# Four of sixteen feed-forward weight products as seven products of 2x2 blocks in a fused transformer layer

## The reference

```
y   = layernorm(x)
sa  = selfattention(y);          a = ln1(y + sa)
ca  = crossattention(a, ctx);    b = ln2(a + ca)
ff  = relu(b @ w1.T + b1) @ w2.T + b2            # 512 -> 2048 -> 512
x   = x + ln3(b + ff)
z   = layernorm(x)
out = x + gate(z) * (relu(z @ W1) @ W2)          # 512 -> 2048 -> 512
```

## Time and profile before

| | |
|---|---|
| median of 3 runs | 531.16 us (529.92 to 531.4) |
| the profiled execution | 530.6 us, span 528.8 us |
| TensorE matmul busy | 518.0 us, 98% of the span |
| VectorE busy | 325.5 us, 62% |
| ScalarE busy | 222.3 us, 42% |
| GpSimd busy | 103.4 us, 20% |

### The profile page before, as it was taken

One profiled execution on the slowest core, in us unless ns is written; L12 is line 12 of the kernel. 1 busy time (PEld: TensorE's weight loads), 2 busy tenths in 40 slices (PEclk: granted clock), 3 DMA queues, 4 the chain that ended last, 5 costly groups with the idle time before them and its releaser, 6 DMA issues.

```text
span 528.8 us, 7550 instructions
## 1 busy us (share of the span) xinstructions
PE 518.0 (98%) x3018; PEld 495.4 (94%) x3018; DVE 325.5 (62%) x558; ACT 222.3 (42%) x388; POOL 103.4 (20%) x92
## 2 busy tenths in 40 slices
PE   7999999999999999999999999999999999999997
PEld 6899999789988878999999999999999899999996
DVE  3743788895698986877365544277684364442225
ACT  3853542383688866264535163206413331320200
POOL 1430430122032135054006300005530000000000
PEclk9999999999999999999999999999999999999999
DMA  8951212031599971229022222002220033100004
GB/s 228 334 187 57 74 64 79 1 113 56 193 292 321 309 219 38 79 96 228 1 77 83 81 81 79 1 0 81 81 79 1 0 126 115 53 28 0 1 1 124
DMA packets 18443, 53.75 MB, mean 102 GB/s; under 512 B 1640, under 2 KB 2440, under 8 KB 15848
## 3 DMA queue, kind: packets, MB, share of 16 engines
q1 hardware_dynamic: 18348, 53.20, 31.2%
q10 hardware_dynamic: 60, 0.07, 0.1%
HBM read 51.63 MB, written 1.64 MB: 101 GB/s over the span
## 4 chain that ended last, share of the span: by engine, by line
PE 81%; DVE 9%; DMA 4%; ACT 3%; issue 1%; SPq 1%; DVEq 0%; ACTq 0%
PE ps L572 21%; PE ps L574 21%; PE ps L573 21%; PE ps L626 3%; DMA OR<-wvo_in 2%; PE ps L602 2%; PE ps L765 1%; DMA cnR<-ctxn_in 1%; PE ps L767 1%; PE ps L766 1%; DMA ctR<-ctxt_in 1%; DVE cnL L1194 1%; PE ps L637 1%; PE ps L739 1%; PE ps L741 1%
## 5 line engine op out<-in xcount | busy, mean ns | idle before, releaser
L572 PE MATMUL ps<-XH,WH 128*128 128x400 f32 x352 | 122.5, 348 | 0.8 <-DVE AL L1206 0.4
L574 PE MATMUL ps<-XH,WL 128*128 128x400 f32 x352 | 121.5, 345 | 0.0
L573 PE MATMUL ps<-XL,WH 128*128 128x400 f32 x352 | 121.4, 345 | 0.0
L572 PE MATMUL ps<-AH,WH 128*128 128x400 f32 x284 | 98.7, 348 | 0.6 <-DVE AL L1210 0.2
L574 PE MATMUL ps<-AH,WL 128*128 128x400 f32 x284 | 98.0, 345 | 0.0
L573 PE MATMUL ps<-AL,WH 128*128 128x400 f32 x284 | 97.9, 345 | 0.0
L572 PEld LDWEIGHTS ps<-XH,WH 128*128 128x128 f32 x352 | 66.1, 188 | 2.7 <-DVE AL L1206 0.8
L573 PEld LDWEIGHTS ps<-XL,WH 128*128 128x128 f32 x352 | 66.2, 188 | 0.0
L574 PEld LDWEIGHTS ps<-XH,WL 128*128 128x128 f32 x352 | 66.2, 188 | 0.0
L484 POOL TENSOR_TENSOR WL<-WR,WH 128x512 fp32r<-128x512 f32 x38 | 52.4, 1410 | 66.6 <-ACT WH L919 66.6
L572 PEld LDWEIGHTS ps<-AH,WH 128*128 128x128 f32 x284 | 53.3, 188 | 2.1 <-DVE AL L1210 1.9
(11 more groups left out here) (188 smaller groups left out, 826.6 us busy)
## 6 DMA issues: line engine op xcount, KB each, us to landing
...
cnR<-ctxn_in SPq DMA_DIRECT2D x8, 256.0 KB
...
VR<-wvo_in SPq DMA_DIRECT2D x4, 256.0 KB, 6.4
```

Of the source, the lines that this page charges most:

```text
L572: pe.matmul(dst, wh, half(mh, h, k), start=(k == 0), stop=False)
L573: pe.matmul(dst, wh, half(ml, h, k), start=False, stop=False)
L574: mm = pe.matmul(dst, wl, half(mh, h, k), start=False, stop=(k == KC - 1))
```

## The change

Four up units (9, 11, 19, 21) are each computed by seven block products instead of eight (the Winograd form of Strassen's scheme). The weights are a 2x2 grid of 256 x 256 blocks, and the tokens' two halves times two feature halves are the other 2x2 grid. POOL makes four sums of weight blocks (`sum_blocks`) for each such unit and, once for each feed forward, four sums of feature blocks (`sum_features`). ACT and DVE split them in high and low parts, at the places that `BLOCKS_AT` and `SUMS_AT` name. One of PE's `strassen(n)` runs 7 products x 2 groups x 6 matmuls; ACT copies the first product out of PSUM, DVE makes the sums of the products in AT and `mid`, ACT writes AH with relu, DVE AL, in the order `HANDED`.

With it go:
- In the first feed forward ORDER becomes 7,0 8,0 7,1 8,1 9 10,0 10,1; before it was 7,0 8,0 9,0 7,1 8,1 9,1 10,0 10,1. The transposes to features of the second half move from after group 0 of 9,0 to after group 1 of 8,0.
- The full-precision normed features are kept in XF, so unit 8's residual is one DVE operation. For the second feed forward eight ACT copies out of PSUM write XF (`copy_features`), and the next transposes or gating rows wait for them.
- The weights of 10, 12, 20 and 22 are split at other places (`MOVED`). POOL's eight additions to the input tokens wait for the end of unit 11 rather than of unit 9. SP's loads of input tokens, g3 and be3 wait for the first four block sums. The load after a block unit waits for its four sums and three low halves.

```diff
-        ORDER += [(_up[0], 0), (_down[0], 0), (_up[1], 0), (_up[0], 1), (_down[0], 1), (_up[1], 1),
+        ORDER += [(_up[0], 0), (_down[0], 0), (_up[0], 1), (_down[0], 1), (_up[1], 0), (_up[1], 1),
...
+STRASSEN = (U_F + 2, U_F + 4, U_M + 4, U_M + 6)
+PRODUCTS = 14
+MOVED = {U_F + 3: POS[U_F + 2, 0], U_F + 5: POS[U_F + 3, 1], U_M + 5: POS[U_M + 3, 1], U_M + 7: POS[U_M + 5, 1]}
...
+BLOCKS_AT = {(U_F, 1): (U_F + 2, [[], [], [0, 1, 2], [3, 4]]), (U_F + 1, 1): (U_F + 2, [[5, 6], [], [], []]),
+             (U_F + 3, 0): (U_F + 4, [[0, 1], [2, 3], [4], [5]]), (U_F + 3, 1): (U_F + 4, [[6], [], [], []]),
+             (U_M + 2, 1): (U_M + 4, [[0, 1], [2], [3], [4]]), (U_M + 3, 0): (U_M + 4, [[5], [6], [], []]),
+             (U_M + 5, 0): (U_M + 6, [[0, 1], [2, 3], [4, 5], [6]])}
+SUMS_AT = {(U_F + 1, 1): (0, [[], [0], [1], [2, 3]]),
+           (U_M + 1, 1): (1, [[0], [1], [2], []]), (U_M + 3, 0): (1, [[], [], [3], []])}
+HANDED = [(0, 0), (0, 1), (0, 2), (0, 3), (1, 2), (1, 3), (1, 0), (1, 1)]
+WHOLE = [n for n in LOADED if n not in STRASSEN]
...
+        def blocks(n, i):
+            if i >= 4:
+                x = n == U_M + 6
+                return [w[x][:, i - 4, :, :] for w in (WXH, WXL, WXS)]
+            ks, es = [(0, 0), (2, 0), (2, D // 2), (0, D // 2)][i]
+            return [w[SLOT[n]][:, ks:ks + 2, es:es + D // 2] for w in (WH, WL, WS)]
+        def raw_block(ks, es):
+            return WR[:, 2 * ks:2 * ks + 2, es * D // 2:(es + 1) * D // 2]
+        def sums(t):
+            lo, whole = [w[0][:, 2 * t:2 * t + 2, :] if t < 3 else w[1][:, :, :] for w in (TL, TS)]
+            return TH[:, 2 * t:2 * t + 2, :], lo, whole
+        def product(n, i, e):
+            return gemm_count(n, 0, 2 * i + e)
...
+            sp.wait_ge(block_sum, 4)
...
+            def sum_blocks(n):
+                pool.wait_ge(weights_loaded, 16 * LOADED.index(n))
+                if BEFORE[n] is None:
+                    pool.wait_ge(c_attT, B)
+                    pool.wait_ge(ct_low, 2 * B)
+                else:
+                    pool.wait_ge(gemm_done, gemm_through(BEFORE[n]))
+                if n == U_F + 4:
+                    pool.wait_ge(gemm_done, gemm_through(U_F + 2))
+                done = 4 * STRASSEN.index(n)
+                a11, a12, a21, a22 = raw_block(0, 0), raw_block(1, 0), raw_block(0, 1), raw_block(1, 1)
+                s2, s3, s1, s4 = [blocks(n, i)[2] for i in range(3, 7)]
+                pool.tensor_tensor(s1, a21, a22, ALU.add).then_inc(block_sum, 1)
+                pool.wait_ge(block_sum, done + 1)
+                pool.tensor_tensor(s2, s1, a11, ALU.subtract).then_inc(block_sum, 1)
+                pool.wait_ge(block_sum, done + 2)
+                pool.tensor_tensor(s4, a12, s2, ALU.subtract).then_inc(block_sum, 1)
+                pool.tensor_tensor(s3, a11, a21, ALU.subtract).then_inc(block_sum, 1)
+            def sum_features(f):
+                if f == 0:
+                    pool.wait_ge(x_ready, 24)
+                else:
+                    pool.wait_ge(x_copied, 2 * KC)
+                b11, b21 = XF[0][:, 0:2, :], XF[0][:, 2:4, :]
+                b12, b22 = XF[1][:, 0:2, :], XF[1][:, 2:4, :]
+                t2, t3, t4, t1 = [sums(t)[2] for t in range(4)]
+                pool.tensor_tensor(t1, b12, b11, ALU.subtract).then_inc(feature_sum, 1)
+                pool.wait_ge(feature_sum, 4 * f + 1)
+                pool.tensor_tensor(t2, b22, t1, ALU.subtract).then_inc(feature_sum, 1)
+                pool.wait_ge(feature_sum, 4 * f + 2)
+                pool.tensor_tensor(t4, t2, b21, ALU.subtract).then_inc(feature_sum, 1)
+                pool.tensor_tensor(t3, b22, b12, ALU.subtract).then_inc(feature_sum, 1)
...
-            split_weights(U_F + 2)
+            sum_blocks(U_F + 2)
+            sum_features(0)
+            sum_blocks(U_F + 4)
             pool.wait_ge(xres_loaded, 32)
             pool.wait_ge(gb_loaded, 32)
-            pool.wait_ge(gemm_done, gemm_count(U_F + 2, 1, KC - 1))
+            pool.wait_ge(gemm_done, gemm_through(U_F + 4))
...
+            sum_features(1)
+            sum_blocks(U_M + 4)
+            sum_blocks(U_M + 6)
...
+                    elif pn in STRASSEN:
+                        if e < 2:
+                            pe.wait_ge(before_relu, 8 * STRASSEN.index(pn) + e + 3)
+                        else:
+                            pe.wait_ge(two_summed, 2 * STRASSEN.index(pn) + e - 1)
...
+            def strassen(n):
+                at = STRASSEN.index(n)
+                pn, ph = ORDER[POS[n, 0] - 1]
+                f = int(n >= U_M)
+                def b(h, k):
+                    return XH[h][:, k:k + 2, :], XL[h][:, k:k + 2, :]
+                moving = [b(0, 0), b(0, 2), sums(0), sums(1), sums(2), sums(3), b(1, 2)]
+                for i in range(7):
+                    ah, al = blocks(n, [0, 1, 3, 4, 2, 5, 6][i])[:2]
+                    bh, bl = moving[i][:2]
+                    for e in range(2):
+                        dst = ps[:, [4, 0, 2, 6, 0, 4, 6][i] + e, 0:HALF]
+                        if e == 0:
+                            pe.wait_ge(block_low, 7 * at + [1, 2, 4, 5, 5, 6, 7][i])
+                            if 2 <= i < 6:
+                                pe.wait_ge(feature_low, 4 * f + i - 1)
+                            else:
+                                pe.wait_ge(x_ready, 24 + 8 * f)
+                        if i in (0, 3) and f == 1:
+                            pe.wait_ge(g_shift, 2)
+                            pe.wait_ge(g_rows_sb, 2)
+                        if i in (0, 3) and at >= 1:
+                            pe.wait_ge(before_relu, 8 * at)
+                        elif i == 1:
+                            pe.wait_ge(dve_evac, dve_count(pn, ph, e))
+                        elif i == 2:
+                            pe.wait_ge(dve_evac, dve_count(pn, ph, 2 + e))
+                        elif i == 4:
+                            pe.wait_ge(before_relu, 8 * at + e + 1)
+                        elif i == 5:
+                            pe.wait_ge(first_copied, 2 * at + e + 1)
+                        elif i == 6:
+                            pe.wait_ge(three_summed, 2 * at + e + 1)
+                        cols = slice(e * P, (e + 1) * P)
+                        for k in range(2):
+                            pe.matmul(dst, ah[:, k, cols], bh[:, k, :], start=(k == 0), stop=False)
+                            pe.matmul(dst, ah[:, k, cols], bl[:, k, :], start=False, stop=False)
+                            mm = pe.matmul(dst, al[:, k, cols], bh[:, k, :], start=False, stop=(k == 1))
+                        mm.then_inc(gemm_done, 1)
...
-            unit(U_F + 1, 0)
-            unit(U_F + 2, 0, [0])
+            unit(U_F + 1, 0, [0, 1])
             to_features(2, 1, xn[1])
-            unit(U_F + 2, 0, [1, 2, 3])
-            for n, h in ORDER[POS[U_F, 1]:POS[U_M - 3, 1]]:
-                unit(n, h)
+            unit(U_F + 1, 0, [2, 3])
+            units(ORDER[POS[U_F, 1]:POS[U_M - 3, 1]])
...
+                    if (n, h) in SUMS_AT:
+                        f, here = SUMS_AT[n, h]
+                        for t in here[e]:
+                            act.wait_ge(feature_sum, 4 * f + (3 if t == 0 else 4))
+                            hi, _, whole = sums(t)
+                            act.activation(hi, whole, ACT.Copy).then_inc(feature_high, 1)
+                    if (n, h) in BLOCKS_AT:
+                        m, here = BLOCKS_AT[n, h]
+                        for i in here[e]:
+                            split_block(m, i)
+            def split_block(n, i):
+                at = STRASSEN.index(n)
+                hi, _, src = blocks(n, i)
+                if i < 3:
+                    act.wait_ge(weights_loaded, 16 * LOADED.index(n))
+                    if BEFORE[n] is None:
+                        act.wait_ge(c_attT, B)
+                        act.wait_ge(ct_low, 2 * B)
+                    else:
+                        act.wait_ge(gemm_done, gemm_through(BEFORE[n]))
+                    src = raw_block([0, 1, 1][i], [0, 0, 1][i])
+                else:
+                    act.wait_ge(block_sum, 4 * at + (3 if i == 3 else 4))
+                act.activation(hi, src, ACT.Copy).then_inc(block_high, 1)
+            def strassen(n):
+                at = STRASSEN.index(n)
+                for e in range(2):
+                    act.wait_ge(gemm_done, product(n, 0, e))
+                    act.activation(mid[:, e, :], ps[:, 4 + e, 0:HALF], ACT.Copy).then_inc(first_copied, 1)
+                for p in range(2):
+                    if POS[n, p] in SPLIT_AT:
+                        for k in range(KC):
+                            split_weights(SPLIT_AT[POS[n, p]], k)
+                for i, (h, e) in enumerate(HANDED):
+                    act.wait_ge(before_relu, 8 * at + i + 1)
+                    act.activation(half(AH, h, e), half(AT, h, e), ACT.Relu).then_inc(act_evac, 1)
...
```

(90 more changed lines are left out.)

89 lines of the change are left out of this document (66 added, 23 removed).

## The result

The changed kernel takes 522.83 us (median of 4, 522.34 to 523.88) against 530.65 us (4 runs, 529.92 to 531.4): ratio 0.9857, 95% interval 0.9841 to 0.9873, about 7.6 us faster. The forecast was 525.0 us in a range of 522.5 to 528.5, and 524.45 for the profiled execution, which took 523.1.

A forecast was written before the change was run, and what follows sets the result against it. PE was taken as the bound, busy 518.0 of 528.8 us. Savings of 8.75 less stalls of 1.2 and 1.4 left 6.15 us, so 524.45 from 530.6; with 0.56 for the median, 525.0 us, range 522.5 to 528.5.

The forecast's parts named there:

- What is removed: Four up units: 12 fewer matmuls each at 0.182 us, nothing lost per group, saving 8.75 us.
- Rival three: In the seven-product sets, groups of six in changing banks lose about 0.1 us each, no saving: 530.6 us; chance 0.07.
- Moved transposes free: Transposes moved into 8,0: features are ready in time for 7,1, no stall, 1.5 us to spare.
- First stall: From 7,1 to 8,1: POOL's feature sums and unit 9's block splits delay AL, a 1.7 us wait for 0.48, +1.2 us.
- Set S9: Seven products of unit 9: DVE has 13.4 us of work in 15.3, so PE does not stall.
- 10,0 and 10,1: Down unit 10: bank free 2 us early; the weight chain lands unit 13's weights 6.2 us into unit 11's products.
- S11 with 1.3 us of slack: Seven products of unit 11: DVE's lateness stays hidden; beyond 1.3 us more it would cost one for one.
- Second stall: Behind unit 11's products, in 13,0: six DVE operations take turns with POOL's token additions, delaying a bank, +1.4 us.
- Second feed forward: Units 15 to 22: added copies, feature sums and block operations stay hidden; nothing added, bound 0 to 1 us.
- rival one: Both stalls mostly hidden because POOL shares rather than locks, or its operations are shorter: 523.0 us; chance 0.17.
- Rival two: DVE is later inside the seven-product sets through the weight chain, 2 to 3 us more: 527.5 us; chance 0.18.
- rival four: POOL's block sums on strips run two to three times their row and cover a set: slower, 537.6 us; chance 0.05.

The follow-up runs named there:

- e6: Changed kernel with the first product of each seven-product set computed twice into the same bank, so 96 matmuls per set; 530.96 us, ratio 1.0008.
- e5: Kernel before with only the new order of the first feed forward's units and the moved transposes, all products ordinary; 531.35 us, ratio 1.0010.
- e3: Changed kernel with unit 9's block splits moved from the end of 7,1 into the first three groups of 8,1; 523.06 us, ratio 0.9855.
- e7: Changed kernel with the load of unit 13's weights waiting for the third group of unit 11's products; 525.35 us, ratio 0.9899.
- e1: Changed kernel with POOL's eight additions to the input tokens waiting for the first group of 14,0; 521.96 us, ratio 0.9829.
- e2: Changed kernel with POOL's eight additions of 512 columns made sixteen of 256, in place; 522.70 us, ratio 0.9852.

## Why the prediction was right, and where it was off

Forecast and result have the same sign and mechanism; the gain was put at 6.15 us and is 7.25 in the stretch, 7.5 between the profiled executions and 7.8 between the medians. Point by point:

- *What is removed*, 8.75 us at 0.182 us a matmul, nothing per group: right. Sets of 15.34, 15.33, 15.33 and 15.31 us, and e6 gives it back. Rival three (0.1 us per group) falls.
- *Moved transposes free*: right (e5).
- *First stall, +1.2 us*: mis-sized, measured +0.34. The step that failed is "it waits to 256.0 and ends at 256.6". I let POOL's four sums start 0.4 us late and added DVE's turns in full; the two sums that meet an AL took 2.13 and 2.25 us, with 1.91 alone, so 0.2 to 0.3 per turn and not 0.57. They end 0.27 us after the AL of group 2 could start, where I had 0.95. Each of the three AL asks in the last 0.2 to 0.3 us of a sum and takes 0.65 to 0.68 us. That the groups (2.19 us) and the sums run in step like this I had not forecast. My own bound without POOL, +0.55, had the right cause (e3) and was 0.2 too high.
- *Set S9, no stall*, and *10,0 and 10,1*: right, though the 13.3 us of DVE in S9 are not the operations of the forecast's 13.4 (see above). The weight chain put unit 13's copies at 6.2 us into S11; they start at 303.69, 5.8 in.
- *S11 with 1.3 us of slack*: 0.4 too small; e7's 2.7 us of delay made 0.99 us of wait, so 1.7.
- *Second stall, +1.4 us by six turns*: right, 1.24, and the cause is shown by e1 and e2. That the size came so near is partly luck: the six operations took 3.10 + 3.28 + 2.99 = 9.4 us and not 6 x 1.886 = 11.3, while the two AT (1.17) and the acc (0.56) that stand between them in DVE's queue, 1.7 us, are missing from the sum. The bank is empty at 27.5 us after S11's start, the sum had 27.6.
- *Second feed forward, nothing added*: right; both sets run without a gap, S19 beside POOL's sums for S21.
- *Which rival*: by its number the result (522.8) is rival one's 523.0, but its reason, sharing instead of turns, is refuted by e2; one stall was as forecast and the other nearly absent. Rival two is real beyond the slack, as e7 shows, but not at today's timing. Of rival four there is no sign: the block sums take 1.28 to 1.74 us, not two to three times their row. Those over 1.5 us, which I had named as a sign of being wrong, made no gap in a set.
- The rest of the difference between medians, 0.3 to 0.6 us, lies ahead of the first feed forward or in the runs' own spread.
